# Eight score tiles of batch 0 from fp32 operands kept on chip, weights as second transfer, new orders

## The reference, cut to what matters

```python
xn = layernorm(x)
q = xn @ Wq + bq; k = xn @ Wk + bk; v = xn @ Wv + bv   # 16 heads of q; 4 of k and v, each serves 4 q heads
attn = softmax((q @ k.T) / sqrt(8))                    # per head, 256 x 256
x = x + (attn @ v) @ Wo + bo + ffn(xn)
```

## Time and profile before

| | us |
|---|---|
| median of 3 runs | 389.63 (389.58 to 389.66) |
| the profiled execution | 391.72 |
| its span, first to last instruction | 389.9 |
| PE busy in it | 379.4 (97%) |
| ACT busy | 310.1 (80%) |
| DVE busy | 304.6 (78%) |
| POOL busy | 251.5 (64%) |
| mean granted TensorE clock | 0.995 of full speed |

### The profile page before, as it was taken

One profiled execution on the slowest core, in us unless ns is written; L12 is line 12 of the kernel. 1 busy time (PEld: TensorE's weight loads), 2 busy tenths in 40 slices (PEclk: granted clock), 3 DMA queues, 4 the chain that ended last, 5 costly groups with the idle time before them and its releaser, 6 DMA issues.

```text
span 389.9 us, 5957 instructions
## 1 busy us (share of the span) xinstructions
PE 379.4 (97%) x1864; PEld 194.0 (50%) x1864; DVE 304.6 (78%) x510; ACT 310.1 (80%) x528; POOL 251.5 (64%) x289
## 2 busy tenths in 40 slices
PE   8999999999999999999998999999999999999996
PEld 6866644545454454243333444743445544464445
DVE  5566879786678969839879988997899989596850
ACT  3622568878868987799999899999949998999550
POOL 4134234547153320435699993999999999999781
PEclk9999999999999999999999899999999999999999
DMA  6276437424552730300000000000000000000000
GB/s 198 58 162 140 125 104 141 99 61 103 162 117 52 136 57 3 110 0 2 1 0 0 3 0 0 2 27 1 1 0 2 0 27 2 0 2 1 23 4 29
DMA packets 28255, 19.03 MB, mean 49 GB/s; under 512 B 2880, under 2 KB 27328, under 8 KB 27968
## 3 DMA queue, kind: packets, MB, share of 16 engines
q1 hardware_dynamic: 28224, 18.65, 19.8%
HBM read 13.46 MB, written 4.98 MB: 47 GB/s over the span
## 4 chain that ended last, share of the span: by engine, by line
PE 47%; issue 25%; ACT 14%; POOL 10%; DVE 3%; POOLq 0%; ACTq 0%; DVEq 0%
POOL acc L1183 7%; PE bank L353 7%; PE bank L446 6%; PE bank L338 5%; PE bank L324 5%; ACT da L1057 5%; PE bank L384 4%; PE bank L878 4%; PE bank L392 4%; ACT pt L528 2%; DVE hb L1135 1%; PE bank L903 1%; ACT L1057 1%; PE bank L452 1%; PE bank L427 1%
## 5 line engine op out<-in xcount | busy, mean ns | idle before, releaser
L1183 POOL TENSOR_TENSOR acc<-acc,hb 128x512 f32<-128x512 f32 x128 | 158.1, 1272 | 16.7 <-DVE hb L1135 11.0
L1135 DVE TENSOR_TENSOR_SCAN hb<-da,bank 128x512 f32<-128x512 f32 x128 | 146.6, 1202 | 23.9 <-PE bank L839 18.6
L569 DVE TENSOR_REDUCE mx<-bank 128x2 f32<-128x512 f32 x128 | 83.2, 684 | 23.4 <-PE bank L324 21.4
L528 ACT ACTIVATE pt<-bank 128x512 f32<-128x512 f32 x128 | 71.6, 595 | 20.3 <-PE bank L338 18.8
L1057 ACT ACTIVATE da<-dt,nega 128x510 f32<-128x510 f32 x128 | 82.1, 715 | 0.2
L878 PE MATMUL bank<-gelu,ld 128*128 128x512 f32 x128 | 59.5, 606 | 0.7 <-ACT gelu L1038 0.7
L866 PE MATMUL bank<-sil,ld 128*128 128x512 f32 x128 | 59.3, 595 | 0.0
L338 PE MATMUL bank<-q_st,k_st 51*128 51x512 bf16 x128 | 42.3, 383 | 1.7 <-ACT pt L528 1.3
L324 PE MATMUL bank<-k_st,q_st 48*128 48x256 bf16 x256 | 42.5, 273 | 0.2
L878 PEld LDWEIGHTS bank<-gelu,ld 128*128 128x128 f32 x128 | 24.7, 194 | 28.4 <-issue 26.8
L866 PEld LDWEIGHTS bank<-sil,ld 128*128 128x128 f32 x128 | 23.7, 190 | 25.4 <-issue 24.8
(11 more groups left out here) (141 smaller groups left out, 575.3 us busy)
## 6 DMA issues: line engine op xcount, KB each, us to landing
q_st<-q_scr SPq DMA_DIRECT2D x8, 384.0 KB, 4.7
q_st<-q_scr SPq DMA_DIRECT2D x15, 192.0 KB, 3.8
ld<-in_pack SPq DMA_DIRECT2D x2, 1024.0 KB, 6.1
q_scr<-qk_parts SPq DMA_DIRECT2D x8, 192.0 KB, 2.1
k_st<-k_scr SPq DMA_DIRECT2D x15, 96.0 KB, 4.0
q_scr<-qk_parts SPq DMA_DIRECT2D x8, 128.0 KB, 2.0
out<-x SPq DMA_DIRECT2D x8, 128.0 KB, 1.9
ld<-in_pack SPq DMA_DIRECT2D x1, 968.0 KB, 5.3
```

Of the source, the lines that this page charges most:

```text
L528: act(pt[:, n % 8, :], st(b, n)[:, :], ACT.Exp, scale=HD ** -0.5).then_inc(p_ok, 1)
L569: eng.tensor_reduce(mx[:, 2 * pair:2 * pair + 2, q], s_bank[n % 2][:, :].rearrange("p (h k) -> p h k", h=2), AX.X, ALU.max).then_inc(mx_ok, 1)
L1135: eng.tensor_tensor_scan(hb[:, s % NPAIR, c, :], da(n).rearrange("p b n -> p (b n)"), b_bank(g, s)[:, :], 0.0, ALU.mult, ALU.add).then_inc ...
L1183: TT(acc[:, g % 2, c, :], acc[:, g % 2, c, :], hb[:, s % NPAIR, c, :], ALU.add).then_inc(add_ok, 1)
```

## The change

1. `project(0)` gets a third fp32 matmul, into bank 2, with a new weight block: Wk with each 8-column key head repeated for its 4 query heads (128 columns). `wide_out` (ACT, new) adds the biases and writes fp32 copies of these wide keys (`kx`) and of the queries (`q_all`) of batch 0.
2. `own_keys` (ACT, new, four calls) writes for two heads each a copy of `kx` in which all partitions but the head's eight are zero. It scales by a column of `own`, a 0/1 table that comes with the constants.
3. The first eight S of batch 0 are now one fp32 matmul of 512 columns over all 128 partitions, `q_all` against two masked copies. They need no transfer. `fetch(0)` reads only what the second eight need.
4. The buffer of the weights `head` grows from 384 to 512 columns and is issued as second transfer instead of fourth; the constants grow from 330 to 347 columns and are third.
5. `NWARM` falls from 96 to 44, and the orders of all engines are new. `first_split` and `xn_transposes(1)` wait for `kx_ok` too.

```diff
@@ ORDERS (each engine has a new list) @@
-    tensor="""20*warm xn_transposes 7*warm project 5*warm ffn_in 3*warm xn_transposes v_gate 3*warm project warm ffn_in
+    tensor="""9*warm xn_transposes warm project 6*warm v_gate 3*warm S ffn_in S warm ffn_in xn_transposes 2*S warm S
...
-NWARM = 96
+NWARM = 44
-for _n in (P, P, NKV * HD, VG, 1, 1):
+for _n in (P, P, NKV * HD, VG, 1, 1, 1, NH):
...
+    q_all, kx = t["dt"][:, 0, 0, 0:T], t["dt"][:, 0, 0, T:2 * T]
+    k_own = t["hb"].rearrange("p s c (e n) -> p (s c) e n", e=2)
...
             if b == 0:
-                k_rows(0, 1).then_inc(sc_ok, 16)
-                q_rows(0, G).then_inc(sc_ok, 16)
-                k_rows(1, NKV).then_inc(sc0_ok, 16)
-                q_rows(G, NH // 2).then_inc(sc0_ok, 16)
+                k_rows(NKV // 2, NKV).then_inc(sc0_ok, 16)
...
         def scores(n):
+            if b == 0 and n < NH // 2:
+                eng.wait_ge(own_ok, pair + 1)
+                reached(eng, mx_ok, b, NH, n - 1)
+                mm(s_bank[n % 2][:, :], q_all[:, q * P:(q + 1) * P],
+                   k_own[:, pair, :, :].rearrange("p e n -> p (e n)"), start=True, stop=True).then_inc(s_ps, 1)
+                return
...
-            if b == 0 and n == G:
-                eng.wait_ge(sc0_ok, 32)
+            if b == 0 and n == NH // 2:
+                eng.wait_ge(sc0_ok, 16)
...
         def project(b):
             mm(bA[:, 0:T], wq[:, :], xnT[b % 2][:, :], start=True, stop=True)
+            if b == 0:
+                mm(st_bank[0][:, 0:T], wkx[:, :], xnT[b % 2][:, :], start=True, stop=True)
...
+        def wide_out(n):
+            eng.wait_ge(ld_cst, 16)
+            reached(eng, qk_ps, 0, 1, 1)
+            act(kx, st_bank[0][:, 0:T], ACT.Identity, bias=bkx_c[:, 0:1]).then_inc(kx_ok, 1)
+            act(q_all, bA[:, 0:T], ACT.Identity, bias=bq_c[:, 0:1]).then_inc(kx_ok, 1)
+
+        def own_keys(pair):
+            if pair == 0:
+                eng.wait_ge(kx_ok, 2)
+            for e in range(2):
+                last = act(k_own[:, pair, e, :], kx, ACT.Copy, scale=own[:, 2 * pair + e:2 * pair + e + 1])
+            last.then_inc(own_ok, 1)
...
         def first_split(b):
             reached(eng, qk_ok, b, 1, 1)
+            eng.wait_ge(kx_ok, 2)
```

More of the change, by code:

```diff
@@ L72 @@
 ORDERS = dict(
-    sync="""x_in constants0 x_in head x_in ffn_weights 3*put fetch stack 3*put fetch put stack 2*put 3*rows fetch loads
-        2*put 3*rows loads put stack fetch rows put 2*rows put stack put fetch 3*rows stack 3*put fetch loads
-        3*rows stack 3*put fetch 3*rows 3*put fetch stack 3*rows stack 3*rows loads 8*out landed""",
-    tensor="""20*warm xn_transposes 7*warm project 5*warm ffn_in 3*warm xn_transposes v_gate 3*warm project warm ffn_in
[L77 to L94, removed]
-        2*b 2*second b out second b 2*second b second step_in b step_in b third b third b 3*third 2*b 3*third
-        ffn b ffn b out ffn b ffn b 2*out b out 3*second b 2*second b 2*second b second b 2*out third b 2*third
-        b third b 4*third 6*out""",
@@ L121 @@
-    gpsimd="""ones 2*biased 8*G 2*qk_split maxima_split 8*G qk_split maxima_split 8*G biased maxima_split qk_split 8*G
-        maxima_split constants G qk_split 7*G maxima_split 3*G qk_split 5*G maxima_split qk_split 8*G
-        maxima_split 8*G maxima_split 2*start split 9*add 2*start 9*add split 13*add y 5*add y start 6*add start
-        8*add split 14*add y 4*add y 8*add start 3*add start 7*add split 11*add y 4*add y 26*add y add y""",
+    sync="""x_in head constants0 2*x_in ffn_weights 3*put fetch stack 3*put fetch 2*put 3*rows loads put stack fetch
+        3*put 3*rows loads stack fetch put rows put 2*rows put stack fetch loads 3*rows put stack 2*put fetch
+        3*rows stack 3*put fetch loads 3*rows stack 3*put fetch 3*rows stack 3*rows 8*out landed""",
@@ L125 @@
+    gpsimd="""ones biased G biased 4*G qk_split 3*G biased qk_split maxima_split 8*G qk_split maxima_split 8*G qk_split
+        maxima_split constants 8*G maxima_split 3*G qk_split 5*G maxima_split 3*G qk_split 5*G maxima_split
+        qk_split 8*G maxima_split 8*G maxima_split 2*start split 12*add start 2*add split 10*add start 11*add y
+        add y start 6*add start 8*add split 14*add y 4*add y 8*add start 3*add start 7*add split 11*add y 4*add
+        y 26*add y add y""",
 )
@@ L171, in layer0 @@
     warm_in = sb("warm_in", [P, 384], BF16)
-    sb("spare", [P, 1106 - NT])
+    sb("spare", [P, 1106 - NT - P])
     pt = sb("pt", [P, 8, 512])
@@ L1252, in program @@
         early = early_buffers(sb)
+        t["hb"], t["dt"] = early["hb"], early["dt"]
         with ExitStack() as only0:
@@ L1298 @@
     host["x"] = l0["x"].reshape(NT, P, P).transpose(1, 0, 2)
[L1299 removed]
+    host["head"] = _np.concatenate([eye, l0["Wq"]] + [l0["Wk"]] * 4
+                                  + [l0["Wk"][:, k * HD:(k + 1) * HD] for k in range(NKV) for _ in range(G)], axis=1)
     host["cst"] = _np.concatenate([l0["Wo"], every(l0["bo"]), every(l0["bv"]), l0["Wv"], l0["ffn_Wg"],
[L1301 removed]
+                                   column(l0["bq"]), _np.tile(l0["bk"], 4)[:, None],
+                                   _np.repeat(l0["bk"].reshape(NKV, HD), G, axis=0).reshape(P, 1),
+                                   _np.repeat(_np.eye(NH, dtype=_np.float32), HD, axis=0)], axis=1)
     host["w12"] = _np.concatenate([l0["ffn_w1"], rows(l0["ffn_w2"])], axis=1)
```

82 lines of the change are left out of this document (51 added, 31 removed).

## The result

The changed kernel takes 384.17 us (median of 4 runs, 383.92 to 385.91), the kernel before 389.61 beside it (4 runs, 389.39 to 389.66). That is 5.4 us less; the ratio is 0.985 with an interval of 0.982 to 0.988. The forecast was 386.1 with a range of 383.4 to 388.8. The time lies in the range, but nearer to rival (a), 384.8, whose condition is what happened: the clock rose in time. One run of one variant (e11) took 395.44 us at a mean clock of 0.973; it is left out of that variant's median.

The account below looks back on a forecast made before the run. The prediction took PE as full from 60 us, behind a head that is a chain of latencies up to A(0). 4.0 - 1.2 + 0.4 gave 3.2, 3.6 with 4.4; 3.5 taken from 389.63 gave 386.1, range 383.4 to 388.8.

Parts of the forecast that it names:

- rival (a): Start of the kernel: the clock rises on time, gain 4.8, 384.8 us (383 with the first scan early); chance 0.27.
- Steps 1 to 5: Head, from projection to A(0): A(0) at 36.0 instead of 40.35, 4.4 earlier, taken as 4.0; POOL's split delays maxima_split 0.5.
- step 4: DRAM trip for the second eight tiles: ninth tile at 22.9 against about 28.5, 5.6 earlier, 0.9 of it waited for.
- Step 6: PE's clock at the start: a wait for xn puts off its rise; cost 0 to 2.6, taken as 1.2.
- Step 7: Behind A(0): four warm calls fewer gain 0.4; permuted later orders, bounds -1.8 to +1.8, taken as 0.
- the first route: Head up to A(0), worked out mark by mark: 4.4 earlier; a second route gave 3.5.
- (b): Second eight tiles, tile 17 and A(0): new waits replace the old, 2.8 of 3.5 gone, 388.9; 0.15 together with (d).
- (c): PE from the projection on: the clock stays at its lower level, slower, 391.3 if until 20 us; chance 0.11.
- (d): First eight tiles: own_keys or the maxima hold them, then everything as in (b); chance 0.15 together with (b).

Follow-up runs that it names:

- e11: e8 with PE's list from 15 to 39 us shortened, all tiles over DRAM, none on chip: 387.57 us, ratio 0.994.
- e9: The changed kernel once more, no edit: 384.23 us, in two groups.
- e4: The kernel before with the early projection alone (9 warm calls ahead of xn's transposes, weights as second transfer): 390.51 us, ratio 1.001.
- e7: The changed kernel with the transfers in the order before (input, constants, input, weights, input): 385.45 us, in two groups.
- e3: The changed kernel with two warm calls ahead of the first transposes instead of nine: 386.72 us.
- e5: The changed kernel with inverse1 on DVE one scan call (two scans) earlier: 383.42 us.
- e12: e10 with a tenth warm call ahead of the first transposes and PE's list between tile 8 and the first A shortened: 383.35 us.
- e6: The changed kernel's orders up to the first A and E, from there the orders of the kernel before: 385.83 us, ratio 0.989.
- e10: e5 with the product -mean x rstd moved from VectorE to POOL, VectorE only negating rstd: 382.81 us, ratio 0.982.
- e1: The kernel before once more, no edit: 389.64 us.
- e8: The kernel before with the early projection alone, eleven warm calls ahead of the transposes, ACT's and POOL's lists mended: 389.21 us, ratio 0.998.

## Why the prediction was right or wrong

- **Steps 1 to 5** had the chain right, and A(0) at 36.0 came at 35.44. Against the profile shown it is 4.9 earlier (4.4 worked out, 4.0 taken); 1.04 of that is the profile's own late clock, so like with like it is 3.9. That 3.9 meets the 4.0 is in part luck: A(0) came 0.6 earlier than worked out, and the profile that it was held against was 1.04 late. own_keys took 0.43 each (0.48 taken), the last put took 0.43 to issue instead of 1.45, and the trip was done before PE came to it: the 0.9 of waiting in step 4 did not come. From max_rows to A(0) took 4.87, 4.7 forecast, but not by the wait that the step named. POOL's maxima_split starts 1.10 after max_rows, against 0.81 before, 0.3 of the 0.5 forecast; and the last of its rows, issued at 33.0, lands 1.8 later, at 34.8. A(0) then stands behind PE's own list, which runs without a gap up to it, six fillers from 34.68 on last.
- **Step 6, the clock, is the step that failed.** It took 1.2, the middle between a rise on time and a late one, on a gap of "more than 1 us". The gap was 0.44, since xn came 0.6 earlier, and both profiles of the changed kernel (after, e9) had the rise in time (6.6 and 6.9 us), as the times of seven of its ten runs suggest: 0. Waits of 0.83, 1.04 and 3.44 (e4, e7, e3) gave late rises, in all three profiles; e3 measured 2.5 for it. The length of the wait is not all that decides: in e5 and e12 PE waited 0.76 and 0.65 with the clock already up, and in the kernel before, with PE fed throughout, it rose at 7.10 in one execution and at 4.87 in another. What sets that is open. Behind the wrong choice stands a sum: fillers ending at 5.2 and xn at 6.27 from the profile of before, whose nmr (L560) of 0.64 us stood beside a sum of POOL; it took 0.16 after the change, since POOL's sums start later. The forecast took over the 0.64 as if it were the instruction's own.
- **Step 7** took 0.4 and measured 1.24: 0.50 from A(0) to first E (0.93 before, 0.43 after: the gate's work moved ahead of it) and 0.74 behind. e6 shows both as the orders'. "Taken as 0" for the permuted orders was the second error. Against e6 they gained 2.3 us between first E and the first scan and gave 1.5 back up to the 33rd, 1.0 of it by one small product (2.25 where e6 has 1.22). e10, which takes that product off VectorE, starts that scan 2.3 earlier. Neither the gain at the change of layers nor that wait is in the forecast, which had bounds of -1.8 to +1.8 there.
- **The sum**: 3.9 + 0 + 1.24 = 5.1 where 4.0 - 1.2 + 0.4, with a little from the first route, made 3.5. Medians give 5.4; e1's profiled execution was 0.36 below its kernel's median.
- **Rivals**: (a) was right in its condition and 0.6 too high in time. (b) didn't come: the ninth tile at 21.86, tile 17 at 30.77 and A(0) have no wait in front of them on PE. (c) is excluded: the projections from 6.96 on run at full speed, and the column shows 1.00 in every stretch up to 370 us. (d) didn't come: the first tile ran at 10.69.
- What the shares are: from e1 to after, first E comes 4.4 earlier. By first E, the early projection with its clock gives 0.9 (e8), a shorter list 1.8 (e11), the tiles on chip 0.8 on top (e6), the new orders 1.0 (after). Medians of the runs without the fall at 215 us, 389.5, 389.0, 387.5, 385.7 and 384.2, give the same four steps 0.5, 1.5, 1.8 and 1.5. So the tiles on chip are worth 0.8 to 1.8 of the whole, less what e11's slip takes; where their share ends and that of the orders starts is not settled, since in e6 the old orders hold back A(0) and first E (max_rows is 2.0 ahead of e11's). Between two and three fifths of the gain need no tile on chip (2.0 of 5.3 by the medians, 2.6 of 4.4 by first E).

## What to carry to other kernels

Look at the head of an engine's list for work that nobody waits for, and move the whole list when its first step moves; an earlier step alone gave 0.4 us here (e8), with the list behind it shortened 2.0 (e11). Before you work out a gain from one profiled execution, take a second one: 2.4 of the 7.6 us between the two spans were the clock of that one execution. A small instruction whose duration is many times that of its twins elsewhere is a wait, and may be worth more than its size.

## What the runs showed of the hardware that I had not expected

- Two groups of times of one unchanged kernel, 389.2 to 390.0 and 391.3 to 391.9, go with the mean granted clock: 1.00 and 0.995. In the two profiles with that fall (the one first shown and e4's) the clock is at its lower level for 3.4 us from 215.3 us. From 210.0 to 215.3 PE was busy 3.78 us in that execution and 3.79 in the one whose clock stayed up, so what decides between the two is not in the profile; in the changed kernel it was busy 4.52, and there the fall was not seen.
- Matmuls' durations show the level where the column doesn't: 1.22 (e3, e7) and 0.70 (after) for the same projection, all with 1.00 in the column.
- A product of two 128 x 8 operands on VectorE takes 0.17 us where no large sum of POOL runs at its start, and 1.2 to 2.9 beside POOL's back-to-back sums of 128 x 512; it ends within 0.03 us of the end of one of them. Started within 0.1 us of the start of a sum, it ended with that sum (1.21 to 1.24, six profiles); 0.26 to 0.29 into it, with the next (2.23 to 2.25, five profiles); 0.87 into it, with the one after that (2.86, e5). A negation of one 128 x 8 operand took 0.43 in the same place (e10). Scans that read one of their operands from PSUM run beside the sums at 1.13 to 1.2, and a reciprocal of 128 x 8 at 0.17 to 0.18.
